# Graph network on one core: where the preparation of the edge lists and the sender table is computed, and by which engine

## The reference

```python
edge_index = jnp.stack([src, dst])
h = relu(layernorm(x)); x = x + L0(h, src, dst)                       # three rounds of mean over neighbours
h = relu(layernorm(x)); x = x + L1(h, edge_index, edge_attr_16, ...)  # means of edge attributes by src and by dst, MLP
h = relu(layernorm(x)); x = x + L2(h, edge_index, ...)                # attention over the edges of each dst
h = relu(layernorm(x)); x = x + L3(h, edge_attr_4, edge_attr_8, src, dst, node_type_4, ...)
```

## Time and profile before

| what | value |
|---|---|
| median of three runs | 2131.21 us (2128.32 to 2134.73) |
| the profiled execution, its own time | 2126.57 us |
| its span, first to last instruction | 2124.8 us |
| busy, share of the span | DVE 83%, PE 76%, PEld 60%, ACT 52%, POOL 46% |
| mean granted TensorE clock (share of 2.4 GHz) | 0.833 |

### The profile page before, as it was taken

One profiled execution on the slowest core, in us unless ns is written; L12 is line 12 of the kernel. 1 busy time (PEld: TensorE's weight loads), 2 busy tenths in 40 slices (PEclk: granted clock), 3 DMA queues, 4 the chain that ended last, 5 costly groups with the idle time before them and its releaser, 6 DMA issues.

```text
span 2124.8 us, 36111 instructions
## 1 busy us (share of the span) xinstructions
PE 1610.9 (76%) x8603; PEld 1273.5 (60%) x8603; DVE 1753.1 (83%) x5207; ACT 1103.9 (52%) x2865; POOL 977.8 (46%) x969
## 2 busy tenths in 40 slices
PE   4656668999998987455777777778377888788786
PEld 3222248888888974344776676677355555555555
DVE  8999988998998977787687787886767778778776
ACT  2787767888997963011423424245434444444443
POOL 4200001111221200577777777760057777777772
PEclk9887779999999998675978869789668787887878
DMA  5665668868886870343222222220021111111111
GB/s 181 197 192 162 181 196 326 308 225 292 323 305 246 327 261 29 110 109 82 71 76 70 79 73 73 75 64 1 32 70 56 54 56 55 55 55 55 55 55 48
DMA packets 168625, 280.38 MB, mean 132 GB/s; under 512 B 23985, under 2 KB 137272, under 8 KB 158578
## 3 DMA queue, kind: packets, MB, share of 16 engines
q1 hardware_dynamic: 132816, 191.61, 27.1%
q0 software_dynamic: 34368, 85.62, 13.4%
q10 hardware_dynamic: 1250, 0.86, 0.2%
HBM read 224.22 MB, written 53.79 MB: 131 GB/s over the span
## 4 chain that ended last, share of the span: by engine, by line
POOL 32%; DVE 13%; issue 12%; PE 11%; ACT 1%; DMA 1%; DVEq 0%; POOLq 0%; ACTq 0%
POOL G L750 19%; POOL AT L738 6%; POOL SCR L738 4%; PE PS L1995 2%; POOL EI L738 2%; PE PS L1996 2%; PE PS L1971 1%; DVE HOT_R L1252 1%; POOL G L738 1%; PE PS L1886 1%; DVE GROUPED_R L1267 1%; DVE GROUPED_R L1261 1%; DVE SCR L1426 1%; PE PS L1770 1%; PE PS L1947 0%
## 5 line engine op out<-in xcount | busy, mean ns | idle before, releaser
L750 POOL DMA_INDIRECT G<-table,src_idx x415 | 406.0, 978 | 167.3 <-issue 125.9
L2102 PE MATMUL PS<-SCR,OH 128*128 128x256 f32 x830 | 281.9, 504 | 107.8 <-DVE SCR L1723 104.7
L2102 PEld LDWEIGHTS PS<-SCR,OH 128*128 128x128 f32 x830 | 201.4, 252 | 160.3 <-DVE SCR L1723 120.7
L1886 PE MATMUL PS<-ALL_R 128*128 128x256 f32 (+3 forms) x2025 | 265.6, 288 | 22.8 <-DVE ALL_R L1314 8.1
L727 POOL DMA_INDIRECT HOT_R<-group_table,EI x56 | 63.3, 1130 | 467.0 <-PE PS L1850 252.3
L1971 PE MATMUL PS<-RX,OH 128*128 x830 | 178.4, 372 | 130.4 <-DVE SCR L1426 80.2
L1886 PEld LDWEIGHTS PS<-ALL_R 128*128 128x128 f32 (+1 forms) x2025 | 250.5, 189 | 25.6 <-issue 9.6
L1971 PEld LDWEIGHTS PS<-RX,OH 128*128 128x128 f32 x830 | 149.3, 248 | 160.2 <-issue 155.4
L738 POOL DMA_INDIRECT AT<-table,src_idx x208 | 213.8, 1028 | 63.4 <-issue 62.2
L957 ACT COPY SCR<-PS 128x640 f32<-128x640 f32 x83 | 57.5, 692 | 287.7 <-PE PS L2077 287.7
L1846 PE MATMUL PS<-HOT_R,GROUPED_R 128*119 128x448 f32 x776 | 181.9, 374 | 9.3 <-DVE G L1272 8.7
(11 more groups left out here) (430 smaller groups left out, 3883.2 us busy)
## 6 DMA issues: line engine op xcount, KB each, us to landing
ALL_R<-adjacency SPq DMA_DIRECT2D x72, 1600.0 KB, 7.5
adjacency<-ALL_R SPq DMA_DIRECT2D x26, 1600.0 KB, 7.6
AT<-dst_in_block SPq DMA_DIRECT2D x103, 128.0 KB
G<-table,src_idx POOLq DMA_INDIRECT x463, 2.5
AT<-table,src_idx POOLq DMA_INDIRECT x208, 2.9
table<-RX SPq DMA_DIRECT2D x10, 320.0 KB, 2.7
radial_rows<-SCR POOLq DMA_DIRECT2D x4, 512.0 KB, 5.7
SCR<-table,src_idx POOLq DMA_INDIRECT x111, 2.8
```

What stands on the lines that cost most here:

```text
L750: pool.indirect_dma_start(G[:, p, q, :], None, tables[i], bass.IndirectOffsetOnAxis(ap=src_idx[:, VB * k + q:VB * k + q + 1], axis=0)).the ...
L1886: ins = pe.matmul(PS[0:m, n % 2, 0:2 * w], (adj(slot) if slot is not None else first_adj(b))(c, m), both(i % 2, c, w), start=j == 0, stop= ...
L2102: ins = pe.matmul(PS[:, q, 0:MSG], OH[:, p, q, :], view(SCR, M_AT + (p * VB + q) * MSG, [[1, MSG]]), start=True, stop=True)
```

## The change

Five edits.

- GpSimd's two passes in the preparation (`L702`, `L703`) wait for `kinds_ready` in place of `valid_made`, which is gone. The order of the kind fills becomes j = 0 of all groups, then j = 1 of all groups, and only the latter wait for `marks_made`.
- GpSimd's casts and its making and storing of the table (`L706` to `L712`) are gone.
- ScalarE makes the table at the start, after its ten weight loads: four `Abs(bias - iota)` of 128 x 448 and one `Relu(1 - that)` over 128 x 1792, then stores it from its own DMA queue. `L1062` sets a new semaphore for it.
- The loads of attributes by GpSimd wait, from g = 1 on, until the table is stored, as their buffers hold it meanwhile.
- ScalarE casts the two lists of indices in the build, at pair 33, just after the layer norm's blocks. GpSimd's fetches (`L727`) wait for it.

```diff
-        FILLS = attr_fills(range(2)) + [(g, j) for g in range(VG) for j in range(2)] + attr_fills(range(2, VG))
+        FILLS = attr_fills(range(2)) + [(g, j) for j in range(2) for g in range(VG)] + attr_fills(range(2, VG))
...
             for g in range(VG):
                 at = bass.IndirectOffsetOnAxis(ap=tvi[:, g:g + 1], axis=0)
+                if g == 1:
+                    pool.wait_ge(s("groups_stored"), 16)
                 if g == ATTR_RING:
                     pack_block_words()
                     pool.wait_ge(s("fill_turned"), 5)
                 pool.indirect_dma_start(attr_rows(g), None, edge_attrs, at).then_inc(s(f"attrs_in{g % ATTR_RING}"), 16)
 
-            pool.wait_ge(s("valid_made"), 1)
+            pool.wait_ge(s("kinds_ready"), 1)
...
             pool.wait_ge(s("fill_copied_act"), N_FILL)
-            pool.tensor_copy(view(EI, 2 * VW + 3, [[VB, NB]]).bitcast(I32), view(EI, 2 * VW + 3, [[VB, NB]])).then_inc(s("idx_made"), 1)
-            pool.tensor_copy(src_idx[:], EI[:, 0, 0:NV + 1]).then_inc(s("idx_made"), 1)
-            pool.wait_ge(s("idx_made"), 2)
-            for c in range(4):
-                pool.tensor_scalar(view(SCR, HIGH0_AT + c * NSRC, [[1, NSRC]]), iota_h[:, 0:NSRC], bv[:, c:c + 1], None, ALU.is_equal).then_inc(s("groups_made"), 1)
-            pool.wait_ge(s("groups_made"), 4)
-            pool.dma_start(group_table.rearrange("(c p) n -> p c n", p=P), view(SCR, HIGH0_AT, [[NSRC, 4], [1, NSRC]])).then_inc(s("groups_stored"), 16)
...
             pool.wait_ge(s("block_summed"), FIRST)
+            pool.wait_ge(s("idx_made"), 2)
...
             act.wait_ge(s("constants_made"), 11)
+            act.wait_ge(s("scalars_made"), 1)
+            for c in range(4):
+                ins = act.activation(view(SCR, HIGH0_AT + c * NSRC, [[1, NSRC]]), iota_h[:, 0:NSRC], ACT.Abs, bias=bv[:, c:c + 1], scale=-1.0)
+            ins.then_inc(s("groups_made"), 1)
+            act.wait_ge(s("groups_made"), 1)
+            act.activation(view(SCR, HIGH0_AT, [[1, 4 * NSRC]]), view(SCR, HIGH0_AT, [[1, 4 * NSRC]]), ACT.Relu, bias=1.0, scale=-1.0).then_inc(s("groups_made"), 1)
+            act.wait_ge(s("groups_made"), 2)
+            act.dma_start(group_table.rearrange("(c p) n -> p c n", p=P), view(SCR, HIGH0_AT, [[NSRC, 4], [1, NSRC]])).then_inc(s("groups_stored"), 16)
             copy_fills(0, KINDS_AT)
...
+                if j == NORM_FROM + NBLK:
+                    act.copy(view(EI, 2 * VW + 3, [[VB, NB]]).bitcast(I32), view(EI, 2 * VW + 3, [[VB, NB]])).then_inc(s("idx_made"), 1)
+                    act.copy(src_idx[:], EI[:, 0, 0:NV + 1]).then_inc(s("idx_made"), 1)
                 if NORM_FROM <= j < NORM_FROM + NBLK:
                     norm_block(j - NORM_FROM)
...
-            dve.tensor_copy(bv[:], stvi[:])
+            dve.tensor_copy(bv[:], stvi[:]).then_inc(s("scalars_made"), 1)
...
-            dve.tensor_tensor(va, id_part(1), id_part(2), ALU.not_equal).then_inc(s("valid_made"), 1)
+            done(dve.tensor_tensor(va, id_part(1), id_part(2), ALU.not_equal))
...
                     if f == KINDS_AT:
                         pe.wait_ge(s("kinds_ready"), 1)
+                        pe.wait_ge(s("keys_copied"), GA)
+                    if f == KINDS_AT + VG:
                         pe.wait_ge(s("marks_made"), 1)
-                        pe.wait_ge(s("keys_copied"), GA)
```

## The result

The kernel after takes 2166.92 us, the median of 5 runs (2159.5 to 2167.52), beside 2130.5 us for 5 runs of the kernel before (2128.32 to 2134.73). The ratio is 1.0164, with a 95% interval of 1.0146 to 1.0183: the change costs 36 us where a gain of 3.5 was forecast. The profiled execution took 2166.79 us, its span is 2165.0. One execution of the run with the scales at visit 16 took 4652.38 us and one of the kernel before beside it 4479.39; both count as slow, and the medians and ratios given here leave them out.

A forecast was written before the change was run, and what follows sets the result against it. VectorE's 590 visits were taken to bound the build, held up by GpSimd's arithmetic. Gains of 1.37 + 2.84 less 0.69 make 3.52 us, so 2131.21 - 3.5 = 2127.7 us, range 2121 to 2134.

The forecast's parts named there:

- L702 and L703 moved: Preparation: VectorE's kinds, no longer slowed by GpSimd's two passes, lose 0.96 and 0.41 us; the moments start 1.37 us earlier.
- A hold of up to 3.32 us: Preparation: upper bound on what GpSimd's two moved passes could cost VectorE's bn_stats; the forecast took nothing.
- The casts and the table off GpSimd: Build: nine slowed visits between 56.84 and 63.80 us return to 0.392 us each; 2.84 us come off.
- The table on ScalarE: Start: ScalarE, idle until 38.74 us, makes the table; its store starts by 13 us and lands at about 17.
- the wait for its store: Preparation: GpSimd's new wait ahead of the attribute load at 32.44 us, 15 us after the table lands, costs nothing.
- the kept second table load: Build: ScalarE still loads a function table ahead of the square root; one load serving both would be 0.69 us better.
- the earlier keys: Preparation: keys keep their time, copied at 47.03 us, so kind fills and square root come 1.05 us earlier, not 1.37.
- The square root late by 0.69 us: Build: VectorE reaches visit 12 at 58.19 us, the root is done at 58.88; a new wait of 0.69 us.
- The sum of 3.52 us: Whole kernel: 1.37 + 2.84 - 0.69 us gained, all on the path, as L1231 follows VectorE's last visit.
- The step that failed: Build: GpSimd's four L715 issues stay beside the visits, costed at nothing either way (0 to 0.2 us, half a visit).
- the first three: Rivals: late tail or held statistics, 2129.4 or 2130.3 (0.17); one table load, 2127.0 (0.08); late table, 2137.7 (0.03).
- Rival 4: After the build: the granted clock comes back at another time, giving 2134.0 or 2121.4 us; chance 0.10.

The follow-up runs named there:

- the run with four comparisons: Changed kernel with GpSimd's four 128 x 448 comparisons put back ahead of the radial rounds, results unused: 2129.18 us, ratio 1.0006.
- the run with SyncE's stores: Changed kernel with the four stores of radial rows issued by SyncE in place of GpSimd, which keeps the loads: 2153.66 us, ratio 1.0115.
- the table alone: Kernel before with only the table moved to ScalarE; GpSimd keeps the casts, L702 and L703: 2168.76 us.
- the early plain DMA: Changed kernel with one more plain DMA, a 512-byte store issued by GpSimd at about 4 us: 2167.47 us, ratio 1.0188.
- one comparison in mid-run: Changed kernel with GpSimd waiting for visit 20, then making one unused 128 x 448 comparison ahead of the radial rounds: 2169.91 us.

## Why the prediction was wrong

Point by point, by its own steps:

- *L702 and L703 moved: 1.37 us.* Right. L1189 takes 0.43 and L1190 0.68; the bn_stats start at 46.69, 1.31 us earlier, and sixteen of them take 3.18 us with GpSimd's two passes beside them (3.17 before). A hold of up to 3.32 us, given as a bound, didn't come. The prediction tried the rule on two SBUF inputs (the Trainium skill's page "SBUF — State Buffer", section "Who interferes with whom") on L1184 alone, which doesn't show it. L1183, which has two such inputs as well, took 1.09 us beside L703 and takes 0.68 without it (L1190), so one of the two rows agrees.
- *The casts and the table off GpSimd: 2.84 us.* The visits did come to 0.396 us each (0.392 was taken), twelve in a row from 53.56 on, and the last one 3.58 us earlier. As far as VectorE goes this term is right.
- *The table on ScalarE, the wait for its store, the kept second table load, the earlier keys.* Right: 5.72 to 11.09 us, no wait ahead of the load at 32.44, a load again at 57.47, the keys 0.24 us earlier only. The casts on ScalarE take 0.34 and 0.53 us and delay nothing (the bound should have been 2.77 / 5 = 0.55, not 0.54). The rule of the Trainium skill's page "ScalarE activation tables: per-element evaluation and per-set limits", section "Table sets in the compiler and the runtime", as the prediction read it, isn't what the trace shows: one load at the start didn't serve the root. That section of the Trainium skill has the loads placed "per block", which the prediction left out, so this speaks against its reading and not yet against the rule.
- *The square root late by 0.69 us.* Right: 0.62.
- *The sum of 3.52 us.* Right for VectorE's last visit, and where neither a held issue nor GpSimd's comparisons are in the way it reaches the hand-over: 3.34 us with the radial rows loaded before the build, and 4.17 with the square root's wait taken out too, where the terms say 3.52 + 0.69 = 4.21.
- ***The step that failed*** is the sentence "the four issues of L715 stay; I cost that at nothing either way (0 to 0.2 us, half a visit)". It priced what an issue costs VectorE, and put at nothing, without asking, what VectorE's visits cost an issue. The step looked at L715, whose slowing of half a visit it had priced, and not at the stores L717 in the same rounds, nor at who waits for them: VectorE itself, after its last visit, ahead of L1231. So the sum's "all on the path, as L1231 follows VectorE's last visit" left out the wait that came last. One store was held for 227.43 us, and three rounds then ran alone: 39.64 us of waiting.

The rivals missed it in the same way: the first three asked what the moved work would delay, and none of the four what the removed work had kept going. The prediction's own picture pointed there. It read the nine slow visits beside GpSimd's arithmetic as a pure loss of VectorE, and didn't ask what that let GpSimd do. Rival 4, the clock that comes back at another time, isn't what cost the 36 us, but it took 3.1 us in the profiled execution of the run with the rows loaded early.

The Trainium skill's page "SBUF — State Buffer", section "SBUF: two separate sides", warns that a DMA issued from GpSimd's queue needs GpSimd to write its descriptors, that certain VectorE instructions lock GpSimd out of a shared port pair meanwhile, and that a DMA issued from ScalarE's or SyncE's queue isn't touched. The runs agree on who is held (GpSimd's issues and, at 226.27 us, its comparison) and who isn't (SyncE's and ScalarE's stores). No run shows that this lock is what holds GpSimd. The Trainium skill's section "Who interferes with whom" of that page has the lock last for one instruction; here a hold outlasted some 1150 of them, and before the scales the same instructions let GpSimd through.

What is shown: that VectorE's visits hold GpSimd (it goes free with one bn_stats, with a stop of VectorE, with the last visit), and that without GpSimd's four comparisons the way is open ahead of the scales and closed behind them, wherever these stand (visits 12, 16, 40). With the comparisons running across the scales it stays open, in the kernel before and in the run with four comparisons that nothing reads. Each run has one profile; that the way closes behind the scales at visit 40 rests on one run alone.

What stays open is why. The length of the comparisons goes a long way with it: on average 246 to 254 and 313 to 319 ns ahead of the scales, where issues pass; 235 or 236 and 305 in every stretch in which GpSimd is held; 248 and 317 behind the scales in the run with four comparisons (66 to 104 us), where all issues pass (the expectation of the run with the scales at visit 40 overlooked this); and 251 and 319 again behind VectorE's stop of 16.03 us in the run with SyncE's stores. But around the stores at 71.00 and 82.25 in the kernel before they take 236 and 305 too, and both pass, so the length doesn't tell the two forms apart. Nor was it tried which instruction of the scales does it.

Open too is why the next stage's clock differs. Over the 15 profiles of this case that stage falls into two groups: 503.6 to 505.4 us in nine, 506.2 to 507.0 in six, and from step 28 to step 32 it takes 23.1 to 23.2 us in each of the nine and 24.3 to 24.5 in each of the six. The six are the runs with the table alone, the early plain DMA, SyncE's stores, one comparison in mid-run, and the rows loaded early and stored by SyncE or by ScalarE. GpSimd stores the radial rows in three of them, so who stores them doesn't decide; nor does the start, which lies between 302.2 and 345.3 us in the six and between 301.3 and 342.9 in the nine; nor the idle time, which is 7.56 us in the run with four comparisons, one of the nine. What does order them is how early the copy of step 4 comes: 21.12 to 21.55 us after the start in the six, 21.57 to 22.42 in the nine; whether that is a cause isn't shown. With one profile of each run it isn't shown whether a kernel keeps to one group.

## What to carry to other kernels

Before taking work off an engine because it slows another, list what else stands in that engine's queue behind it, and who waits for that: the slowing may be the price at which the rest gets through. A long unbroken run of VectorE's short instructions can starve GpSimd to its end, as here for 227.43 us, so DMAs that GpSimd must issue belong ahead of it, or on another engine's queue if that queue can wait for their data without harm. When a row of the changed profile has a mean that no neighbour has (57284 ns against 570), start there.

## What was unexpected

An issue of GpSimd, 0.57 us elsewhere, held for 191 to 227 us by instructions of 0.24 and 0.31 us; a comparison held for 226.27 us in the same way; and one bn_stats of 0.28 us enough to let a single issue go, while the next one was held again for 151.68. And 3.34 us won at a hand-over were all but lost again in the next stage of that execution, though TensorE's wait ahead of the slower stretch was only 0.17 us longer (7.35 against 7.18): its clock stood at 0.50 and 0.83 where it had been 0.65 and 0.99.
